# Full attention written out unit by unit, with a ring of four exponent banks and one of three maxima banks

## What is computed

```python
scores = jnp.einsum('bthd,bshd->btsh', q, k) * scale
probs = jax.nn.softmax(scores, axis=2)
context = jnp.einsum('btsh,bshd->bthd', probs, v)
```

## Time and profile before

| | us |
|---|---|
| median of 3 runs | 3747.01 |
| lowest and highest | 3736.17, 3747.88 |
| profiled execution | 3746.78 |
| its span, first to last instruction | 3745.0 |

### The profile page before, as it was taken

The page is one execution under the profiler, slowest core; times in us unless marked ns, Lnnn a source line. Parts: engine busy times, 40 slices in busy tenths (PEclk is TensorE's granted clock), DMA queues, the critical chain, the costliest instruction groups (busy, mean ns, idle before and its releaser), DMA issues. The chain is left out here.

```text
span 3745.0 us, 56124 instructions
## 1 busy us (share of the span) xinstructions
PE 3316.6 (89%) x18410; PEld 1673.7 (45%) x18410; DVE 2784.8 (74%) x4210; ACT 2237.7 (60%) x3978; POOL 956.6 (26%) x906
## 2 busy tenths in 40 slices
PE   7848898887999979896869999999999999977896
PEld 3327777776666647674312222222222222214664
DVE  6639999997666645454678888888888888834665
ACT  5659999997000002221238888888788888872342
POOL 7539999995000000001210000000000000001000
PEclk9979999999999989998969999999999999997998
DMA  3446434412111120202310000000000000001001
GB/s 129 171 136 185 118 97 102 102 50 76 50 54 53 36 62 1 70 12 72 91 44 14 20 18 20 14 22 14 21 14 21 14 20 16 11 18 57 23 22 45
DMA packets 187750, 198.15 MB, mean 53 GB/s; under 512 B 66962, under 2 KB 134162, under 8 KB 186708
## 3 DMA queue, kind: packets, MB, share of 16 engines
q1 hardware_dynamic: 187492, 194.79, 18.3%
HBM read 127.38 MB, written 67.37 MB: 52 GB/s over the span
## 5 line engine op out<-in xcount | busy, mean ns | idle before, releaser
L1721 DVE TENSOR_REDUCE attn_part_max<-attn_pM 128x1 f32<-128x1024 f32 x1024 | 1204.8, 1219 | 165.1 <-PE attn_pM L1776 161.9
L1701 ACT ACTIVATE attn_probs<-attn_pE 128x512 f32<-128x512 f32 x2048 | 1090.2, 597 | 207.0 <-PE attn_pE L1825 202.5
L1825 PE MATMUL attn_pE<-attn_q,attn_k_exp 128*128 128x512 bf16 x2048 | 629.5, 386 | 31.6 <-ACT attn_q L1673 24.7
L535 POOL TENSOR_TENSOR scan_dbu<-scan_du,scan_b_all 128x2048 f32<-128x2048 f32 x128 | 578.5, 4553 | 16.0 <-DVE scan_h L594 13.5
L1796 PE MATMUL attn_pA<-attn_probs,attn_v 128*32 128x512 f32 x4096 | 561.1, 605 | 0.0
L594 DVE TENSOR_TENSOR_SCAN scan_h<-scan_abar,scan_states,scan_dbu 128x512 f32<-128x512 f32 x384 | 458.8, 1265 | 0.1
L1825 PEld LDWEIGHTS attn_pE<-attn_q,attn_k_exp 128*128 128x128 bf16 x2048 | 139.0, 97 | 609.1 <-ACT attn_probs L1701 462.7
L608 PE MATMUL scan_hT<-scan_ident,scan_h 128*128 128x128 f32 x2048 | 323.4, 281 | 71.2 <-ACT scan_hcT L546 29.4
L559 ACT ACTIVATE scan_abar<-scan_delta,scan_decay 128x512 f32<-128x512 f32 x512 | 372.1, 727 | 18.2 <-DVE scan_h L594 18.1
L546 ACT ACTIVATE scan_hcT<-scan_hT,scan_c_t 128x512 f32<-128x512 f32 x512 | 367.1, 717 | 1.5 <-PE scan_hT L608 1.4
L1775 PE MATMUL attn_pM<-attn_k_exp,attn_q 64*128 64x512 bf16 x1024 | 326.7, 392 | 35.2 <-DMA attn_k_exp<-mid_k_parts 18.6
(11 more groups left out here) (274 smaller groups left out, 3841.4 us busy)
## 6 DMA issues: line engine op xcount, KB each, us to landing
scan_b_all<-mid_BC SPq DMA_DIRECT2D x32, 1024.0 KB, 9.9
attn_q<-mid_q_parts SPq DMA_DIRECT2D x224, 64.0 KB, 2.4
mid_gT<-front_gT SPq DMA_DIRECT2D x8, 1024.0 KB, 7.6
mid_uT<-front_uT SPq DMA_DIRECT2D x8, 1024.0 KB, 9.1
mid_dT<-front_dT SPq DMA_DIRECT2D x8, 1024.0 KB, 4.3
scan_delta<-mid_dT SPq DMA_DIRECT2D x8, 1024.0 KB, 7.6
scan_u_in<-mid_uT SPq DMA_DIRECT2D x8, 1024.0 KB, 9.8
scan_g<-mid_gT SPq DMA_DIRECT2D x8, 1024.0 KB, 5.5
```

Source lines behind the costliest of these rows:

```text
L535: nc.gpsimd.tensor_tensor(dbu[:, G % NDBU, :, :], du[:, u % 2, :, :], b_row, ALU.mult).then_inc(dbu_ready, 1)
L1701: nc.scalar.activation(probs[:, kt % 4, h, :], pE[:, bank(item), :], ACT.Exp, scale=SCALE).then_inc(exp_done, 1)
L1721: nc.vector.reduce_max(part_max[:, h, j, i:i + 1], pM[:, m % 2, :], AXIS_X).then_inc(max_read, 1)
L1825: nc.tensor.matmul(pE[:, bank(item), :], k_exp[:, par, kt * 128:(kt + 1) * 128], q[:, qc, h, :], start=True, stop=True).then_inc(e_psum, 1)
```

## The change

- `pE` gets four banks (EB = 4), `pM` three banks of 512 keys (MB = 3) instead of four.
- VectorE reduces each half of a maxima pair by itself, so `part_max` has four values for 1024 + 1024 keys instead of two. A maxima pair waits until the first half of the pair before it is read.
- TensorE's order in a tile: all four exponent products (in tile 0 the row of head 3 between the third and fourth), one maxima pair, a row if the tile has one, the sums, the other maxima pair.
- The banks of `pE` are given out over the whole stage in order of use (`USES`, `PLACE`), and all 32 units are written out for all engines. No hardware loop is left in the stage.

The core of the diff:

```diff
-    EB = 3
+    EB, MB = 4, 3
...
-    UNIT = [item for kt in range(KT) for item in step_items(kt)]
-    P_UNIT = len(UNIT)
-    assert P_UNIT % EB == 0
...
+    UNITS = NB * QC
...
-    def bank(item):
-        return UNIT.index(item) % EB
+    USES = [(item, of_unit(item, u)) for u in range(UNITS) for kt in range(KT) for item in step_items(kt) if 0 <= of_unit(item, u) < UNITS]
+    PLACE = {use: i for i, use in enumerate(USES)}
+
+    def bank(item, v):
+
+        return PLACE[item, v] % EB
...
-        part_max = s.sb("part_max", [128, G, 4, 2])
+        part_max = s.sb("part_max", [128, G, 4, 4])
...
-        pM = s.ps("pM", [128, 2, 2 * CH])
+        pM = s.ps("pM", [128, MB, CH])
...
-        def every_bg(eng, body):
-
-            def both(pair, first, last):
-                for par in range(2):
-                    body(pair * 2 + par, pair, par, first and par == 0, last and par == 1)
-            both(0, True, False)
-            with eng.Fori(1, NB // 2 - 1) as pair:
-                both(pair, False, False)
-            both(NB // 2 - 1, False, True)
+        def every_unit(body):
+
+            for u in range(UNITS):
+                bg, qc = divmod(u, QC)
+                body(u, bg, qc, u == 0, u == UNITS - 1)
...
-                with pool.Fori(1, NB * QC) as u:
+                for u in range(UNITS):
                     for h in range(G):
                         split(u, h)
...
-                    dve.wait_ge(m_psum, u * M_UNIT + m + 1)
-                    nc.vector.reduce_max(part_max[:, h, j, i:i + 1], pM[:, m % 2, :], AXIS_X).then_inc(max_read, 1)
+                    n = u * M_UNIT + m
+                    dve.wait_ge(m_psum, n + 1)
+                    for half in range(2):
+                        nc.vector.reduce_max(part_max[:, h, j, 2 * half + i:2 * half + i + 1], pM[:, (2 * n + half) % MB, :], AXIS_X).then_inc(max_read, 1)
...
-                    at_least(pe, max_read, u * M_UNIT + m - 1)
-                    nc.tensor.matmul(pM[:, m % 2, 0:CH], q[0:64, qc, h, j * 128:(j + 1) * 128], k_exp[0:64, par, i * CH:(i + 1) * CH], start=True, stop=True)
-                    nc.tensor.matmul(pM[:, m % 2, CH:2 * CH], q[64:128, qc, h, j * 128:(j + 1) * 128], k_max[64:128, par, i * CH:(i + 1) * CH], start=True, stop=True).then_inc(m_psum, 1)
+                    n = u * M_UNIT + m
+                    qc, par = u % QC, u // QC % 2
+                    at_least(pe, max_read, 2 * n + 2 - MB)
+                    nc.tensor.matmul(pM[:, 2 * n % MB, :], q[0:64, qc, h, j * 128:(j + 1) * 128], k_exp[0:64, par, i * CH:(i + 1) * CH], start=True, stop=True)
+                    nc.tensor.matmul(pM[:, (2 * n + 1) % MB, :], q[64:128, qc, h, j * 128:(j + 1) * 128], k_max[64:128, par, i * CH:(i + 1) * CH], start=True, stop=True).then_inc(m_psum, 1)
...
-                        for kt in range(KT):
-                            items = step_items(kt)
-                            take(items[0])
-                            take(items[1])
-                            if not end:
-                                both_maxima(kt)
-                            take(items[2])
-                            if kt == 0 and not start:
-                                sums(u - 1, KT - LAG, par if qc else 1 - par)
-                            for item in items[3:]:
+                    for kt in range(KT):
+                        late = [item for item in step_items(kt) if item[0] == "row" and kt]
+                        for item in step_items(kt):
+                            if item not in late:
                                 take(item)
-                            if kt == 1 and not start:
-                                sums(u - 1, KT - 1, par if qc else 1 - par)
-                            if kt == LAG:
-                                pe.wait_ge(v_in[par], (pair + 1) * 16)
-                            if kt >= LAG:
-                                sums(u, kt - LAG, par)
...
+                        if not last:
+                            if kt == 0:
+                                next_inputs()
+                            maxima(2 * kt, u + 1)
+                        for item in late:
+                            take(item)
+                        if kt < LAG and not first:
+                            sums(u - 1, KT - LAG + kt, (u - 1) // QC % 2)
+                        if kt == LAG:
+                            pe.wait_ge(v_in[par], (bg // 2 + 1) * 16)
+                        if kt >= LAG:
+                            sums(u, kt - LAG, par)
+                        if not last:
+                            maxima(2 * kt + 1, u + 1)
```

More of the change, by code:

```diff
@@ L1607, in _, with body @@
                 load_v(0, 0)
[L1609 to L1623, removed]
+                def body(u, bg, qc, first, last):
+                    if not first:
+                        sp.wait_ge(e_psum, u * E_UNIT)
+                    if u + 2 < UNITS:
+                        load_q((u + 2) // QC, (u + 2) % QC, Q_ROWS)
+                    if qc == 0 and bg + 1 < NB:
+                        par = (bg + 1) % 2
+                        load_k(bg + 1, par, k_exp, K_LOW, 0, L, kexp_in)
+                        load_k(bg + 1, par, k_max, K_MAX, HALF, HALF, kmax_in)
+                        load_k(bg + 1, par, k_exp, K_HIGH, 0, L, kexp_in)
+                        at_least(sp, pv_done, u * KT)
+                        load_v(bg + 1, par)
+                    if not first:
+                        store(u, (u - 1) // QC, (u - 1) % QC)
                     if last:
-                        store(NB * QC, bg, QC - 1)
-                every_bg(sp, body)
+                        store(UNITS, bg, qc)
+                every_unit(body)
                 sp.wait_ge(ctx_out, 16 * NB * QC)
@@ new lines, in body @@
+                def body(u, bg, qc, first, last):
+                    for kt in range(KT):
+                        for item in step_items(kt):
+                            v = of_unit(item, u)
+                            if not 0 <= v < UNITS:
+                                continue
+                            if item[0] == "e":
+                                h = item[1] % G
+                                act.wait_ge(e_psum, u * E_UNIT + item[1] + 1)
+                                if h == 0:
+                                    at_least(act, pv_done, u * KT + kt - 3)
+                                nc.scalar.activation(probs[:, kt % 4, h, :], pE[:, bank(item, v), :], ACT.Exp, scale=SCALE).then_inc(exp_done, 1)
+                            elif item[0] == "row":
+                                move_row(v, v % QC, item[1])
+                            else:
+                                move_out(v, bank(item, v))
+                        if kt == LAG - 1 and not first:
+                            move_sums(u - 1)
@@ L1739, in _, with body @@
                     take_max(m, 0)
[L1741 to L1747, removed]
-                            if not end:
-                                take_max(2 * kt, u + 1)
-                                take_max(2 * kt + 1, u + 1)
+                def body(u, bg, qc, first, last):
+                    for kt in range(KT):
+                        if kt == OUT_KT + 1 and not first:
+                            take_out(u - 1)
+                        if not last:
+                            take_max(2 * kt, u + 1)
+                            take_max(2 * kt + 1, u + 1)
@@ L1751, in body, with bank_free @@
                     if last:
-                        take_out(NB * QC - 1)
-                every_bg(dve, body)
+                        take_out(u)
+                every_unit(body)
             @block.tensor
             def _(pe):
[L1758 to L1762, removed]
+                def bank_free(item, v):
+                    at = PLACE[item, v] - EB
+                    if at < 0:
@@ L1804, in _ @@
                 for m in range(M_UNIT):
-                    maxima(m, 0, 0, 0)
+                    maxima(m, 0)
                     if m % M_HEAD == 4 and m > M_HEAD:
```

87 lines of the change are left out of this document (41 added, 46 removed).

## The result

| | us |
|---|---|
| before, median of 4 runs beside it | 3745.52 |
| after, median of 4 runs | 3869.13 (3867.42 to 3869.38) |
| ratio, 95% interval | 1.0334 [1.0316, 1.0352] |
| profiled execution, its span | 3867.42, 3865.6 |

The change makes the kernel 3.3% slower. The forecast was 3867.

The account below looks back on a forecast made before the run. TensorE was taken to set the pace. Unit start 67.6, tile 4 17.1, first maxima 9.2, writing out -14.2 and clock 40 sum to 119.7; with 3746.8 that gives 3867 us, range 3812 to 3908.

Parts of the forecast that it names:

- start of a unit: Tile 0: the row waits for the chain from the last maxima pair; 2.18 us more in 31 units, +67.6 us.
- tile 4: A maxima pair waits 0.57 us while VectorE does peak, reciprocal and context product; 30 units, +17.1 us.
- written out: All units of the stage run like the straight-line ones, without the hardware loop: -14.2 us.
- clock: Idle gaps in tile 0 bring TensorE's granted clock down to 0.50: +40 us, ends 0 and 84.
- Order within a tile: Plain tile: 2.59 us against 2.61, still four changes of shape, so nothing counted.
- the other side: Rival: no cost where maxima and sums touch, 102 us less; 3724 if the clock holds, 3765 with falls; chance 0.06.
- first maxima: First unit, at half clock: waits on the first half 8.1 us, with two moved maxima pairs together +9.2 us.
- VectorE is not the bound: Rival that VectorE becomes the bound: halves don't overlap, about 140 us more, near 4000; chance 0.03.
- a fall in three units of four: How often tile 0's gaps bring the clock down, mostly short falls, priced at 1.3 us a unit.
- the clock holds: Rival: tile 0's gaps are too short to bring the clock down, 3746.8 + 79.7 = 3827; chance 0.2.
- Long falls in every unit: Rival: the row's copy keeps TensorE idle into the fall, 84 us for the clock, 3911; chance 0.12.
- Fourth bank for exponents: Exponent products wait for the ScalarE read four places back, not three; TensorE had no wait there, so no gain.

Follow-up runs that it names:

- r2: Kernel after, with eight extra products that nothing reads put ahead of head 3's row in tile 0: 3816.38 us, ratio 1.0198.
- r1: Kernel before with all 32 units written out, its own order and rings kept: 3728.83 us, ratio 0.9977.
- r3: Kernel after, with tile 0's row and fourth exponent product moved behind both maxima pairs and the sums: 3769.38 us, ratio 1.0085.
- r5: Kernel after, with each unit's reciprocal (as power of -1) and context product moved from VectorE to GpSimd: 3844.14 us, ratio 1.0275.
- r4: Kernel after with its new order but the old rings, three banks for exponents and four for maxima: 4032.26 us, ratio 1.0782.

## Why the prediction was right

The terms, as forecast and as the traces have them:

| term | forecast | measured | from |
|---|---|---|---|
| start of a unit and tile 4, per unit | 2.18 + 0.57 = 2.75 | 2.62 | r2's unit 46.60 less r1's 43.98 |
| the same over 30 units | 82.5 | 78.6 | |
| first maxima to first exponent product of unit 1 | 9.2 | 11.6 | 81.47 to 93.12 |
| written out | -14.2 | -14.8 | 30 x (44.473 less 43.98) |
| clock, 30 units | 40 | 51.4 | 30 x (48.313 less 46.60) |
| last unit, from its start to the last context product | +2.2 | -3.4 | 44.63 to 41.20 |
| stage | 119.7 | 123.4 | 1460.3 to 1583.7 |

The one unit of the kernel after without a fall takes 46.69, so 0.09 of a unit in the clock's line belong to the line of the start. Outside the stage 2.8 us were won, which nothing in the change explains, so the spans differ by 120.6.

**Order within a tile.** Right: a plain tile takes 2.61 us in both. With it falls the rival of the other side. Maxima and sums now touch twice a tile, and the sums start 0.32 after the maxima pair (2231.72 to 2232.04), as forecast (0.31). The four changes of shape cost what they cost before.

**Start of a unit, tile 4, first maxima.** Right. The chain of tile 0 lasts 4.57 for 4.55 forecast, tile 4 is 0.59 over for 0.57, and the first unit's maxima go from 35.32 to 43.39 us, 8.1 as forecast. r3 and r5 take them away one at a time, and the time follows: r3's units are 1.44 us shorter than r2's, r5's tile 4 0.59. VectorE is not the bound: its reductions overlap, and behind the first unit TensorE waits for it in tile 4 alone. In its other tiles a unit wins some 0.2 us in all, which the forecast didn't have: tile 1 took 2.67 and several plain ones 2.63 to 2.65, and now they take 2.61. So r2's unit came out 0.13 under the forecast, though its tile 0 costs 2.21 more than before and its tile 4 0.59. The first unit lost 2.4 more than forecast, in its first tiles, which have no sums yet. There the maxima wait for VectorE at half the clock, as the timeline of the kernel after shows:

```profile
1948.15 0.60 PE L1766 MATMUL attn_pM<-attn_k_exp,attn_q 64*128 64x512 bf16 x1
...
1949.54 0.61 PE L1766 MATMUL attn_pM<-attn_k_exp,attn_q 64*128 64x512 bf16 x1 [0.79 <-DVE attn_part_max L1713]
```

The clock came up at 1957.7 of the span instead of 1941.2. The forecast had taken these tiles for plain ones.

**The clock.** The mechanism was right, its size was not. The step that was off is "a fall in three units of four": the clock fell in 30 units of 31. The price of one was near. Units with a short fall take 48.0 to 48.3 us, so one costs 1.4 to 1.7, and a long one 49.4 - 46.6 = 2.8, against 1.35 and 2.7. The 30 units of the table hold 24 short falls and 5 long ones: 24 x 1.55 + 5 x 2.8 = 51.2. The thirtieth lies in the last unit and is in that line. How often the clock falls does not follow from the wait alone: the wait is 2.05 us in all 31 units of the kernel after, of r5 and of r4, and the falls are 30, 28 and 23. What decides was not found. The rival "the clock holds" is refuted by the windows above; what it would have given, r2 shows: 74 us (67 to 81) over its own kernel before, for the rival's 80. "Long falls in every unit" is refuted by the five of thirty.
The Trainium skill ("TensorE: Matmul & The Clock Gate", section "Why this matters for your kernels") warns only of idle gaps between bursts that are longer than the one here. By it a gap of 2.05 us should be safe. The trace says otherwise, 30 times of 31, and the measurement decides.

**Fourth bank for exponents.** "It gains nothing" was wrong in two ways, and this is the step that was argued badly. It looked at the old order alone. In the new one the burst of four needs the fourth bank: without it a tile costs 0.43 more (r4). And in the last unit, which makes no maxima, TensorE had been waiting for banks, at 2.39 us a tile; no row of a middle unit shows that. The timeline of the last unit, of r1 (the old rings) and of the kernel after:

```profile
3314.28 0.82 PE L1821 MATMUL attn_pE<-attn_q,attn_k_exp 128*128 128x512 bf16 x3
3315.36 0.39 PE L1821 MATMUL attn_pE<-attn_q,attn_k_exp 128*128 128x512 bf16 x1 [0.26 <-ACT attn_probs L1697]
```

```profile
3461.39 1.04 PE L1814 MATMUL attn_pE<-attn_q,attn_k_exp 128*128 128x512 bf16 x4
3463.36 1.04 PE L1814 MATMUL attn_pE<-attn_q,attn_k_exp 128*128 128x512 bf16 x4
```

Four in a row 1.97 us apart: the last interval between context products shrinks from 33.01 to 27.35, a gain of 5.7 us that the forecast didn't have. The last unit was thus forecast 5.6 us too long, the units' waits 3.9, and writing out 0.6 too small a gain. These took back 10.1 of the 13.8 by which clock and first unit went over. So the total owes part of its closeness to luck: errors that cancel.

**Written out.** Right in the trace (r1, and every unit of the kernel after alike but for the clock). Timed alone it was 9 us instead of 14.

**Left open.** Why the timed gain of r1 is smaller than the trace's, why about every sixth fall of the clock lasts twice as long, and why the same wait of 2.05 us leaves the clock alone in one unit of 31 here and in 8 of r4's.

## What to carry to other kernels

When instructions are put in another order on an engine that sets the pace, look for the chain over other engines that ends in one of them, and count what stands between its first and its last step: here a chain of 3.2 us went from fully covered to covered by 1.1. A wait of TensorE of a couple of microseconds in each round of a loop is to be priced with the clock that it brings down, which here added 1.7 us to each stall of 2.2, and some work that keeps the engine busy can be worth more than its time. A ring's depth is to be judged in the order that it will serve, and in the last round too, where other work has gone.

## What the hardware showed that was not expected

- Idle 2.05 us and then 0.77, with 0.38 us of work between them, were followed by a granted clock of 0.50 in 30 of 31 units of the kernel after, in 28 of r5's and in 23 of r4's. In r2, with 0.24 in place of the 2.05, it stayed at 1.00 in all.
- GpSimd took 2.90 us to raise 16 values in each of 128 partitions to the power -1, where VectorE's reciprocal of the same values took 0.24.
- Where TensorE waited for GpSimd's split, it started 0.14 us after the split's end, in all 31 units of the kernel after; where it waited for a reduction of VectorE, it started 0.06 us after its end.
